# Packing four small matmul steps of a fused attention, scan and expert kernel, with a new instruction order

## The reference, cut to what matters

```
h = layernorm(attention_a(layernorm(x)))          # 16 heads of 64, one shared k and v, causal, a null key
xz = rmsnorm(h) @ in_proj_w ; x_in, z = split(xz) # 2 x 512 columns
x_in = silu(x_in)
a_mod = sigmoid(x_in @ A_proj_w + A_proj_b)       # the decay projection, 512 columns
B_in = x_in @ B_proj_w ; C_in = x_in @ C_proj_w   # 16 columns each
y = liquid_scan(x_in, a_mod, sigmoid(A_base), B_in, C_in)   # over the 64 tokens
x = x + h + ((y + D * x_in) * silu(z)) @ out_proj_w
q = l2norm(q) * q_scale ; k = l2norm(k) * k_scale # attention c: norms over the 64 numbers of a head
c = layernorm(attention_c(layernorm(x)))          # with relative position biases
logits = c @ gate_w + gate_b                      # 8 experts, the largest is taken
x = x + onehot(argmax(logits)) * (c @ expert_w + expert_b)
```

## Time and profile before

| | |
|---|---|
| median of 3 executions | 1923.5 us |
| the profiled execution | 1921.49 us |
| its span, first to last instruction | 1919.7 us |
| TensorE busy | 1751.2 us, 91% |
| VectorE busy | 1276.9 us, 67% |
| GpSimd busy | 893.5 us, 47% |
| ScalarE busy | 807.7 us, 42% |
| TensorE's share of the chain that ended last | 86% |

### The profile page before, as it was taken

How to read it: one execution, slowest core, us unless ns; L and a number is a source line. 1 busy time by engine, 2 the same in 40 slices (tenths; PEclk the granted TensorE clock), 3 DMA queues, 4 the chain that set the end, 5 groups by cost and what they waited for, 6 DMA issues and landing times.

```text
span 1919.7 us, 37680 instructions
## 1 busy us (share of the span) xinstructions
PE 1751.2 (91%) x11407; PEld 1373.9 (72%) x11407; DVE 1276.9 (67%) x2684; ACT 807.7 (42%) x1943; POOL 893.5 (47%) x552
## 2 busy tenths in 40 slices
...
DMA packets 40185, 26.52 MB, mean 14 GB/s; under 512 B 19786, under 2 KB 38226, under 8 KB 40148
## 3 DMA queue, kind: packets, MB, share of 16 engines
...
## 4 chain that ended last, share of the span: by engine, by line
PE 86%; DVE 4%; issue 3%; ACT 3%; POOL 2%; SPq 2%; DMA 0%; POOLq 0%; DVEq 0%; ACTq 0%
PE bank L715 12%; PE bank L661 12%; PE bank L618 8%; PE bank L620 7%; PE bank L619 7%; PE bank L683 6%; PE bank L795 6%; PE bank L707 4%; PE bank L696 3%; PE bank L810 3%; PE bank L671 3%; PE bank L784 3%; PE bank L644 2%; PE bank L639 2%; SPq L448 2%
## 5 line engine op out<-in xcount | busy, mean ns | idle before, releaser
L1543 POOL TENSOR_TENSOR a_prob<-a_prob,a_mask 128x1024 f32<-128x1024 f32 x32 | 76.2, 2382 | 264.5 <-DVE a_prob L1209 264.5
L1582 POOL TENSOR_TENSOR y<-y,u 128x512 f32<-128x512 f32 x128 | 162.4, 1269 | 54.1 <-DVE u L1331 49.1
L1331 DVE TENSOR_TENSOR u<-bank,Ef 128x512 f32<-128x512 f32 x128 | 88.5, 691 | 135.8 <-PE bank L795 135.8
L1529 POOL TENSOR_TENSOR c_prob<-c_qT 128x1024 f32<-128x1024 f32 x32 | 82.3, 2573 | 160.4 <-ACT c_qT L926 160.4
L1562 POOL TENSOR_TENSOR resid<-xres,a_c 128x256 f32<-128x256 f32 x32 | 23.6, 738 | 267.8 <-DVE x L1339 215.5
L661 PE MATMUL bank<-a_xnT,a_wq 128*128 128x128 f32 x1024 | 129.2, 281 | 10.2 <-DVE gate_w_lo L1417 10.2
L795 PE MATMUL bank<-u,Gm 128*128 128x512 f32 x256 | 130.9, 613 | 7.8 <-DVE Gm L1323 4.5
L661 PEld LDWEIGHTS bank<-a_xnT,a_wq 128*128 128x128 f32 x1024 | 126.0, 198 | 13.3 <-issue 10.4
L1574 POOL TENSOR_TENSOR u<-xe,Ef 128x512 f32<-128x512 f32 x96 | 122.8, 1294 | 0.0
L715 PE MATMUL bank<-c_wo,c_prob 128*128 128x256 f32 x512 | 121.4, 391 | 0.0
L715 PE MATMUL bank<-a_wo,a_prob 128*128 128x256 f32 x512 | 119.1, 386 | 1.7 <-ACT Ef L1050 1.7
...
## 6 DMA issues: line engine op xcount, KB each, us to landing
...
```

Source lines behind the costliest of these rows:

```text
L1331: dve.tensor_tensor(tm[l][:, :], banks[f"b.m{l}"][:, :], Ef[l][:, :], ALU.mult)\
L1529: pool.tensor_tensor(qsq[:, :, :], X.qT[:, :, :], X.qT[:, :, :], ALU.mult)\
L1582: pool.tensor_tensor(y[:, :], y[:, :], tm[l][:, :], ALU.add).then_inc(g.done(f"y{l}"), 1)
```

## The change

- **Decay and B, C projections.** `b.a` and `b.bc` become `b.a0` and `b.a1`. Each multiplies with 256 columns of the decay weights and, beside them, 16 columns of B's (a0) or C's (a1): twice 12 matmuls of 272 columns and one bias matmul. ScalarE makes `ae` in two halves. `b.BC` reads both banks and waits for ae1.
- **Query norms.** `c.qs` takes 8 matmuls whose stationary operand is a selector of 32 columns and whose moving operand is the squares; four of them write side by side to 32 partitions each, in two rounds that accumulate. VectorE clips 128x128 in place of 128x16, a new step `c.qt` transposes, and `qr` is made from its bank.
- **Key norms.** `c.kv` makes the keys with tokens on partitions (64 columns). ScalarE squares and sums them along the free axis in one instruction, VectorE clips one column, ScalarE makes the factor and scales the keys from PSUM (128x128, both halves); a new step `c.kT` transposes them. `c.ks` on TensorE, `kc` and the multiplication `kn` (L1161) on VectorE go.
- **Expert bias.** The one-hot rows stand twice in a tile of 128 columns, so `c.oT` transposes 128x128; `c.eb` is one fp32r matmul of 40 rows, high and low parts of the biases below each other.
- The copy of x1 to c_xin (L1145) goes; the stream uses x1 itself.
- `ORDER` and `TURNS` are written anew; an iteration begins with `c.PT0`.

```
 ORDER = {
     "pe": """
-        ... c.ks@3 c.q0@3 c.q1@3 b.a@2 c.ex2@4 c.qs@3 c.S0@3 c.S1@3
-        b.bc@2 a.PT0@1 a.PT1@1 c.ex3@4 a.xt@0 b.gt@2 b.E0@2 a.O0@1 ...
+        ... c.q0@3 c.q1@3 b.a0@2 b.a1@2 c.kT@3 c.qs@3 c.ex2@4 c.qt@3 c.S0@3 c.S1@3 a.PT0@1 b.gt@2
+        a.PT1@1 b.E0@2 b.E1@2 a.O0@1 ...
 TURNS = {
-    0: c.ks@3>dve.ks b.bc@2>dve.Ct a.xt@0>act.xnT ...
+    0: ... c.kT@3>dve.K1 c.qt@3>act.qr_l b.E0@2>act.E0u b.m0@2>dve.t0
 PE kv:
+                            pe.matmul(bank("kv")[:, 0:DH], X.xnT[:, k, :], X.wkk[:, k, 0, :],
+                                      start=k == 0, stop=k == KD - 1)
-                def ks(t):
-                    pe.matmul(bank("ks")[:, 0:P], const("halves"), ksq[:, :], start=True, stop=True)\
+                def kT(t):
+                    pe.wait_ge(*act.at("kn", t))
+                    pe.transpose(bank("kT")[:, 0:P], kn[:, :, :], ident).then_inc(p.done("kT"), 1)
 PE qs:
-                    for hp in range(HP):
-                        mm = pe.matmul(bank("qs")[:, 2 * hp:2 * hp + 2], qsq[:, hp, :], const("pair"),
-                                       start=True, stop=True)
+                    for r in range(2):
+                        for c in range(4):
+                            mm = pe.matmul(bank("qs")[32 * c:32 * (c + 1), 0:P], const("pairs")[:, 32 * r:32 * (r + 1)],
+                                           qsq[:, 4 * r + c, :], start=r == 0, stop=r == 1)
+                def qt(t):
+                    pe.wait_ge(*dve.at("qs", t))
+                    pe.transpose(bank("qt")[:, 0:P], qss[:, :], ident).then_inc(p.done("qt"), 1)
 PE a, bc:
+                def a(n):
+                        bank = banks[f"b.a{n}"]
+                        for k in range(KE):
+                            product(bank[:, 0:D + NST], xiT, [w[:, k, n, :] for w in w_abc], k, k == 0, False)
+                        pe.matmul(bank[:, 0:D + NST], bias_ones[:, :], a_bias_parts[:, n, :], start=False, stop=True)\
 PE eb:
-                    pe.matmul(banks["c.eb"][:, 0:D], ohT[:, :], b_e[:, :], start=True, stop=True)\
+                    pe.matmul(banks["c.eb"][:, 0:D], ohT[:, :], b_e_parts[:, :], start=True, stop=True)\
 ACT kr:
+                    act.activation(kn[:, :, :], banks["c.kv"][:, 0:DH].unsqueeze(1).broadcast_to([P, 2, DH]),
+                                   ACT.Copy, scale=kr[:, :]).then_inc(a.done("kn"), 1)
 ACT qr:
-                    act.wait_ge(*dve.at("qs", t))
+                    act.wait_ge(*p.at("qt", t))
 DVE BC:
-                    dve.wait_ge(*p.at("bc", t))
+                    dve.wait_ge(*act.at("ae1", t))
```

More of the change, by code:

```diff
@@ L68, in constants @@
     parts["halves"] = half * 1.0
-    parts["pair"] = half[:, [0, DH]] * 1.0
+    pair = np.zeros((P, 2, 32))
+    pair[:, 0, 0:2] = pair[:, 1, 2:4] = half[:, [0, DH]]
+    parts["pairs"] = pair.reshape(P, 64)
     sums, count_b, count_c, masks = [], [], [], []
@@ L105 @@
     "pe": """
[L106 to L110, removed]
+        c.PT0@4 c.PT1@4 b.m2@3 c.eb@5 c.O0@4 c.O1@4 b.m3@3 b.xt@2 c.W@4 a.q0@1 b.yT@3 c.ct@4 b.x@2
@@ L111 @@
+        c.lg@4 b.z@2 b.out@3 c.oT@4 c.ex0@4 c.ex1@4 a.q1@1 a.S0@1 c.xt@3 a.S1@1 b.xiT@2 c.kv@3
+        c.q0@3 c.q1@3 b.a0@2 b.a1@2 c.kT@3 c.qs@3 c.ex2@4 c.qt@3 c.S0@3 c.S1@3 a.PT0@1 b.gt@2
+        a.PT1@1 b.E0@2 b.E1@2 a.O0@1 b.E2@2 a.O1@1 c.ex3@4 b.E3@2 b.G@2 a.W@1 a.xt@0 b.m0@2 b.m1@2
+        a.kv@0""",
     "act": """
-        b.rms@2 c.rstd2@4 b.yT@3 c.cT@4 b.xnT@2 a.q0@1 c.le@4 b.xe@2 b.ze@2 c.oT@4 b.xs@2
-        c.rstd@3 a.q1@1 c.xnT@3 b.zs@2 b.xiT@2 c.ksq@3 a.rstd@0 c.kr@3 c.q0@3 c.q1@3 a.expm@1
@@ L116 @@
     "dve": """
[L117 to L121, removed]
+        b.t1@3 a.c@2 c.out@5 a.K@1 b.t2@3 b.xn@2 b.t3@3 b.yl@2 a.V@1 c.st2@4 a.st@0 c.c@4 c.cl@4
@@ L122 @@
+        c.lg@4 c.oh@4 b.xg@2 b.zg@2 c.ac0@4 b.x1@3 c.st@3 c.mk@3 c.ac1@4 c.xn@3 b.xi@2 a.S0@1 a.S1@1
+        c.ac2@4 b.zi@2 c.ac3@4 b.xl@2 c.ks@3 a.mx@1 a.sub@1 a.mk@0 c.V@3 a.den@1 b.ag@2 c.K@3 c.qs@3
+        b.nh@2 b.BC@2 c.S0@3 c.S1@3 c.ac4@4 c.ac5@4 c.mx@3 c.sub@3 a.xn@0 c.ac6@4 b.Gm@2 c.den@3
+        a.st2@1 c.ac7@4 b.t0@2""",
     "pool": """
-        b.y@3 b.resid@2 a.addm@1 c.qsq@3 a.norm@1 c.addb@3 c.addm@3 b.dx@2 b.u0@2 b.u1@2 b.u2@2
-        c.norm@3 b.u3@2 b.y0@2 b.y1@2 b.y2@2 b.y3@2""",
+        b.y0@3 b.y1@3 b.y2@3 b.y3@3 b.y@3 b.resid@2 b.dx@2 a.addm@1 c.qsq@3 a.norm@1 c.addb@3
@@ L125 @@
+        c.addm@3 b.u0@2 b.u1@2 b.u2@2 c.norm@3 b.u3@2""",
     "sp": """
@@ L394, in build @@
         ksq = sb("ksq", [P, P])
-        kss = sb("kss", [P, P])
         kraw = sb("kraw", [P, P])
-        kr_l = kr = kn = kss
-        qss = sb("qss", [P, H])
+        kn = kraw[:, :].rearrange("p (two n) -> p two n", two=2)
+        kss = sb("kss", [P, 1])
+        kr_l = sb("kr_l", [P, 1])
+        kr = sb("kr", [P, 1])
+        qss = sb("qss", [P, P])
         qr_l = sb("qr_l", [P, H])
```

180 lines of the change are left out of this document (95 added, 85 removed), and 4 rows, old and new, of the table RESULTS.

## The result

| | before | after |
|---|---|---|
| median | 1924.55 us (1917.19 to 1926.11, 4 executions) | 1857.63 us (1854.94 to 1860.49, 4 executions) |
| ratio, with its 95% interval | | 0.966 (0.963 to 0.969) |
| the profiled execution | 1921.49 us | 1859.48 us |
| its span | 1919.7 us | 1857.7 us |
| TensorE busy | 1751.2 us | 1675.2 us |

The forecast was 1857 us. First the steady part, as in the earlier trace rows: a window, and the group of the decay bias matmul, which now comes twice a tile and answers to the earlier trace rows.

What follows compares the result with a forecast made beforehand. TensorE alone was taken to set the steady pace, 54.65 us a tile. A new tile of 52.6 saves 2.05, 64 us over 31 intervals, plus 1 at the end: 1921.5 - 64 - 1 = 1857 us, range 1803 to 1893.

Steps and rivals of the forecast that it cites:

- The work on TensorE: Sum of the changed steps on TensorE: 2.15 us less work a tile, between -1.9 and 3.0.
- A mis-sized term: 272 columns: In b.a0 and b.a1: 0.131 us per matmul of 272 columns, 3.8 us for both halves, a gain of 0.95.
- b.nh and the wait for Ct: VectorE's b.nh no longer falls under c.addb, 0.69 us instead of 2.72; TensorE's wait for Ct goes, gaining 1.1 to 1.3.
- The wait at c.qt: New TensorE wait of 1.2 us a tile: VectorE's c.qs stands behind b.ag, which GpSimd's a.norm holds.
- the two waits are not added, the longer one counts: Waits ahead of c.qt and c.PT0 cover each other; with the former, c.norm ends 0.7 us before c.PT0 is asked for.
- 0.1 for c.PT0: Allowance of 0.1 us a tile for further delay of the softmax chain ahead of c.PT0.
- my 0.5 for c.PT0 without a wait at c.qt: If c.qt did not wait, c.norm would end 0.5 us after TensorE asks for c.PT0.
- No new wait: Rival: b.ag precedes a.norm or the norms' matmuls are cheap, TensorE alone sets a 51.3 us tile; 1816 us, chance 0.27.
- The softmax chain decides: Rival: c.sub is held by GpSimd's u instructions, 1.2 to 2.4 us more before c.PT0; 1888 us, chance 0.17.
- 272 as 512: Rival: matmuls of 272 columns cost as much as 512, TensorE has 3.0 us more a tile; 1910 us, chance 0.05.
- Slower by the clock: Rival: waits at c.qt or c.PT0 grow to some 2.5 us and lower TensorE's clock; 1945 us, chance 0.06.
- The rule on tiling modes: Mode changes drain TensorE: two drains around c.qs would take some of the 1.15 gain back; by the trace, nothing.

Runs made afterwards that it cites:

- e4: The changed kernel's new steps, but in the order and bank turns of the kernel before: 1901.57 us, ratio 0.987.
- e7: B and C apart from the decay projection again, in the changed kernel with both VectorE moves of e3: 1834.78 us.
- e1: The changed kernel with c.K and c.qs moved ahead of b.ag in VectorE's list, nothing else: 1836.16 us.
- e3: The changed kernel with both VectorE moves, c.K and c.qs ahead of b.ag and a.xn ahead of c.mx: 1809.73 us, ratio 0.940.
- e2: The changed kernel with a.xn moved from behind c.sub to ahead of c.mx in VectorE's list, nothing else: 1838.12 us.
- e5: The changed kernel with the old query norms (8 matmuls of 2 columns, no c.qt), order otherwise the same: 1887.51 us.
- e6: The old query norms (8 matmuls of 2 columns, no c.qt) in the kernel with both VectorE moves of e3: 1861.79 us.
- e10: e3 with c.xt moved from between a.S0 and a.S1 to ahead of a.S0: 1805.09 us, ratio 0.938.

## Why the prediction was right, and where it wasn't

**The work on TensorE: right in sum.** 2.15 us less a tile were forecast, 2.24 came. By steps: a0 and a1 a gain of 0.73 instead of 0.95 (below), c.qs 1.19 instead of 1.15, c.qt 0.26 instead of 0.2, c.eb 0.31 instead of 0.3. c.kT gained nothing against c.ks (0.26 against 0.22). Two terms I had put at nothing, or nearly, gave some: the four matmuls for c's keys take 0.48 instead of 0.64, and c.PT0 and PT1 0.93 instead of 1.11; c.oT lost nothing. e4 says that part of the gain belongs to the order rather than to the steps: with the same steps in the old order (53.79 less 1.81 idle) TensorE has 51.98 us of work, 0.7 more than with the new order. So the steps alone gave 1.55 of the 2.24, and the forecast took all of its 2.15 from them. The lower bound of that sum, -1.9, was added up wrongly: its own terms give -2.2.

**A mis-sized term: 272 columns.** I took 0.131 us for one and 3.8 for both halves. Records of 272 columns start 0.125 apart, so that was nearly right, and the two biases took 0.31 each, as taken. But the first records of the halves took 0.21 and 0.24 (the first from 1074.12 to 1074.33) and those ahead of the biases 0.22 (1075.59 to 1075.81), about 0.09 more than I took for a record. Four such places cost 0.36, and 0.13 of it comes back from the other records and the biases: 4.01. e7 fits the price of the whole, since its tile is 0.88 longer, 0.75 by work and 0.13 by the wait at c.ct.

**b.nh and the wait for Ct: right, and e4 shows that it is the order's doing.** 705 ns, and no wait. Where the order is the old one, b.nh is again 2702 ns under c.addb, and TensorE waits.

**The wait at c.qt: the right mechanism, 0.8 instead of 1.2.** b.ag was held by a.norm and c.K and c.qs stood behind it; e1 moves them and the wait is gone. a.norm started for another reason than I gave: not at once after qsq, but 0.94 us later, when a_rden was made (1077.98). qsq itself took 1.90 and not 2.63. From the end of c.q1 (1074.12) the end of a.norm lay at 5.8 (5.6 forecast), and c.qt started at 7.3 (7.1 forecast): that it is so near is luck, for these two errors cancel. TensorE asked for it later than I had it, at 6.5 and not 6.0, 0.3 of it because a0, a1 and kT took longer. The Trainium skill, "SBUF — State Buffer", Who interferes with whom, has the lock that explains this: the one that issues first keeps the shared ports for its whole instruction. The trace agrees, again for b.ag (1433 ns) and now for a.xn (1279). e1 shows it for b.ag: 425 ns by a move within the list alone.

**The step that failed: "the two waits are not added, the longer one counts", with 0.1 for c.PT0.** Here 0.57 us stood ahead of c.PT0 although c.qt had waited 0.81. e1 to e3 show that the waits add up (21.5 and 19.5 us alone, 47.9 together). I had counted that b.nh and Bt, Ct would make VectorE late for the scores, by which c.PT0 would wait 0.5, and that a wait at c.qt would cover this and leave 0.7 to spare. It covers only the lateness of VectorE: with it, VectorE waits for the scores (0.41 us at 1082.92, with b.nh long done), and without it, in e1, c.S1 on VectorE ends 0.39 us later behind the start of the scores. The rest of the wait moves both ends of the race, for the softmax starts from c.S0 on TensorE, which stands behind c.qt. Even the 0.39 us are no gain at c.PT0: in e1 TensorE comes 0.39 us later to it as well, and its wait is 0.58, as with the wait at c.qt.

The chain itself was not longer than I counted. From the end of c.S1 on VectorE (1084.40) to the end of c.norm (1098.01) it takes 13.6 us, against the 14.35 that I took from before. c.addb and c.addm take 4.85 instead of 5.29, and ScalarE's c.prob follows 0.07 us behind c.sub and not 1.35. But between the end of c.prob (1093.17) and c.den (1094.25) there are 1.08 us that were not there before: a.xn, which the new order put between c.sub and c.den and which falls under u, with c.ac6 and b.Gm behind it. I had looked for such a hold at c.sub, which isn't stretched (1.22), and not at the operation behind it. Without this one c.PT0 would not have waited, which e2 shows. So my 0.5 for c.PT0 without a wait at c.qt was nearly what e1 measures (0.58), and what failed is the step that took it away.

So errors met that cancel: the first wait was 0.4 too large, the second 0.5 too small, and a wait of 0.2 at c.ct was missing. Waits of 1.3 were forecast and 1.6 came, and the work was 0.1 better. The tile gained 1.96 us over the 31 intervals and not 2.05. From one profiled execution to the other 65 us were forecast and 62 came; that the median of 1857.6 meets the forecast to 1 us is also because it lies 2 us below the profiled execution. The precision is luck in good part. The range did not depend on it.

**The rivals.** *No new wait* was priced at 1816 with a tile of 51.3; e3, which has neither of the two waits, takes 1809.7 with 51.24, so the price was nearly right, and it took two moves within the list to get there. *The softmax chain decides* was half of the truth: it decides beside the wait at c.qt, by 0.57 a tile, and by a.xn under u and not by c.sub. *272 as 512* is out (0.125 apart, and 512 columns 0.246). *Slower by the clock* did not occur in this kernel: the clock was 1.00 in the window. But e5 and e6 show a trigger that I had not looked at: not a wait of TensorE, but a stretch in which it is busy, with the 16 narrow records of the old c.qs at its end. In the new order the old norms would have cost 29 us of clock (e5), and the new ones avoid that. This part of the new norms' worth I had not seen at all.

**The rule on tiling modes: I gave it too little.** I wrote that the scores leave no gap that I could see. The Trainium skill, "TensorEngine Tiling (Array Packing)", Key Properties, says that changing the mode drains TensorE. The runs have a cost, though a small one, and whether it is a drain they don't show: c.kT takes 0.26 ahead of the 32-column c.qs (e3: 1098.35 to 1098.61) and 0.17 ahead of the full-width one (e6: 1017.99 to 1018.16), with the same instruction ahead of it. The moving operands of the two also differ in width, 128 columns and 2, so this pair alone doesn't prove it. e10 gains 0.08 on the scores and 0.09 on the tile by one change into and one out of the 64-column mode less. In the sum it is c.kT's term, which I had at 0.17.
